# Moving the experts' final sum to ScalarE and GpSimd, one mask product to GpSimd, and the gate selectors of the first norm to a later place

## The chip, the cores and the metric

The kernel runs on one core of a Trainium2 chip. The metric is the device time of one execution in microseconds. TensorE (PE), VectorE (DVE), ScalarE (ACT), GpSimd (POOL) and SyncE (SP, which issues DMAs here) each run their own instructions in program order; they are held together by semaphores alone, so where a wait stands in an engine's order decides what queues behind it.

## The reference

The input is eight images of 32 channels by 64 by 64 pixels. What is computed, cut to what matters:

```python
xn = norm_w * instance_norm(layernorm_over_channels(x)) + norm_b
q, k, v = split(qkv_w @ xn + qkv_b)                  # 4 heads of 8, windows of 8 x 8 pixels
x = x + proj_w @ softmax(q k^T * 8**-0.5) v + proj_b
t = tokens(x)                                        # (8, 4096, 32)
n = layernorm_over_channels(t)
p, i = top_k(softmax(n @ router_w + router_b), 2)    # 2 of 8 experts
p = p / sum(p)
t = t + sum_k p[k] * (n @ expert_w[i[k]] + expert_b[i[k]])
```

The kernel multiplies each token by the gate of each expert (zero for the six that are not chosen) and sums the experts in PSUM.

## The kernel before

The 32768 pixels are cut in 16 chunks of 4 images by 512 pixels; a partition holds a channel of an image. Four chunks make a quad. There are three stretches.

**Start (0 to about 60 us).** All of x is loaded by five transfers on SP's queue, the weights by three and the gate selectors `gate_sel` by a fourth on ACT's queue. For each quad, PE subtracts the channel mean (L547), ACT squares, PE forms variances (L470), ACT takes roots (L508), DVE inverts them (`reciprocals_first`, L1085), PE spreads them over the channels (`piece_spread`, L482), and DVE multiplies (`first_norm`, L515, four instructions) and takes statistics (`statistics`, L1055). Ahead of the first quad's `first_norm` DVE runs `selectors` (L1102): it waits for `gate_sel`, and makes `regroup` (L1104), `sel_sum` (L1107) and `centre_rep` (L1112, four copies). PE uses `regroup` and `sel_sum` only at L723, after the last quad. PE then waits for `biases_ready` (L729), which DVE raises after copying three results out of PSUM bank 7 (L1133 to L1136), and begins the chunks of attention.

**Attention (about 60 to 289 us).** For every chunk PE makes scores (L596), DVE takes their maximum and subtracts it (L1149, L1152), PE turns them (L609), ACT exponentiates (L894), PE weighs the values (L626). Chunk 0 holds no earlier chunk's work. In its first half PE's order is scores, queries of chunk 1 (L566), keys of chunk 1 (L571), two turns, and only then the scores of the second half (second L596). The queries need `x_cur` of chunk 1, which ACT makes after `instance_deviation(1)` (L1000); that one waits for DVE's moments of the second group of images.

**Experts (about 289 us to the end).** For each chunk c and each half eh of the experts:

- PE makes gates for four images, two at a time (`gate_pair`, L751, banks 2 to 5) from `gate_rows`. The first pair of a chunk waits for `gates_in[c % 4]`, which stands for the transfer of that quad's gates.
- ACT copies bank 2 (`copy_gates`, L1008); POOL multiplies the first image's tokens by it (`scale`, L413); DVE multiplies the second's (L1289) and the last two's (L1292) straight from PSUM.
- PE sums the experts (`experts`, L760) in bank 6 or 7, upon the bias (L772). At eh = 0 it runs `experts(c - 1, 1)`; at eh = 1 `experts(c, 0)`. In between stand the replication of tokens for two chunks on (L737) and, in chunks 0 to 5, norms and logits for quads 2 and 3.
- DVE adds the finished sum of chunk c - 1 to the tokens (`combine`, L1267) after its two multiplications of (c, 0), and writes `out_sb`.
- The gates of quads 2 and 3 are worked out meanwhile in 30 numbered steps: DVE does most (`HALF_STEPS`), POOL 6, 14, 22, 23, 26, 27 and 29 (`LATE_POOL`), ACT the exponential, 25 and 28. Step 20 is L1226, step 21 L1228, steps 22 and 23 are L376 and L378 on POOL, step 24 is L1232 on DVE. Quad 2 takes chunks 2 to 5, quad 3 chunks 6 to 9.

SP's order in this stretch is this, and no part of the change touches it:

```python
for c in range(CHUNKS):
    if c + 3 < CHUNKS:
        repeat_tokens(c + 3)                 # 8 transfers
    if c % QUAD == 2 and c // QUAD + 1 < QUADS:
        move_gates(c // QUAD + 1)            # 4 transfers; gates_in
    sp.wait_ge(summed, c + 1)
    sp.dma_start(out_v[:, c // BANDS, c % BANDS, :], out_sb[:, c % 2, :]).then_inc(stored[c % 2], 16)
```

`summed` is raised by `combine`. So the transfers of iteration c wait until `combine(c - 1)` is done.

Of the kernel before, what the change touches and what calls it, by code (L numbers as in the profile page):

```python
# [6 lines left out]
B, C, H, W = 8, 32, 64, 64  # L7
HEADS, WS, E = 4, 8, 8
# [32 lines left out]
def metaformer_block(nc, io):  # L41
# [3 lines left out]
    with ExitStack() as ctx:  # L45
# [21 lines left out]
        v_cols = sb("v_cols", [P, 2, NW * IMG * HALVES, 2, 2, D])  # L67
        v_flat = v_cols[:].rearrange("p u g b n d -> p (u g b n d)")
        squares = sb("squares", [P, QUAD, CHUNK])
        probs = sb("probs", [P, 4, CHUNK])  # L70
# [119 lines left out]
        pool_scaled = sem("pool_scaled")  # L190
        y_step = sem("y_step")
        summed = sem("summed")
        stored = [sem(f"stored{u}") for u in range(2)]
# [54 lines left out]
        for quad in range(EARLY, QUADS):  # L248
            for h, n in ((1, 6), (4, 14), (6, 22), (7, 23), (8, 26), (8, 27), (9, 29)):
                LATE_POOL[late_half(quad, h)] += [(quad, n)]  # L250
# [51 lines left out]
        def _(pool):  # L302
# [104 lines left out]
            def scale(c, eh):  # L407

                if eh == 0:
# [4 lines left out]
                                   ALU.mult).then_inc(pool_scaled, 1)  # L414

            for c in range(CHUNKS):
                for eh in range(2):
                    h = 2 * c + eh
                    late = [(q, n) for q, n in LATE_POOL[h]]
                    for quad, n in late:  # L420
                        if n == 23:
                            gates(quad, n)
                    scale(c, eh)
                    if h == 0:
                        early(CHUNKS, 0)
                    if h == 2:
                        early(CHUNKS, 1)
                    if h == 3:
                        early(CHUNKS + 1, 0)
                    for quad, n in late:  # L430
                        if n != 23:
                            gates(quad, n)
# [86 lines left out]
        def _(pe):  # L519
# [81 lines left out]
            def turn(n, v):  # L601

                if v % 2 == 0:
                    pe.wait_ge(shifted_done, n * 4 + (v // 2 + 1))
                pe.wait_ge(exp_done, n * NW + (v + 1))
                unit, hh = v // 2, v % 2
                for b in range(IMG):
                    heads = shifted_unit[:, unit % 2, b, HALVES * hh:HALVES * hh + HALVES, :]
                    last = nc.tensor.transpose(bank[TURN_BANKS[v % 2]][:, b * P:b * P + P],  # L609
                                               heads.rearrange("p h k -> p (h k)"), const["c_ident"][:, :])  # L610
                last.then_inc(turned_ps, 1)
# [116 lines left out]
            values(0)  # L728
            pe.wait_ge(biases_ready, 1)  # L729
            chunk(0, 0, first=True)  # L730
# [34 lines left out]
            def bias(c):  # L765

                wait_past(pe, summed, c - 1)
                if c == 1:
                    pe.wait_ge(x2_done, CHUNKS + X2)
                quad = c // QUAD  # L770
                pe.wait_ge(gate_step[quad], GATE_OPS + ONE)
                nc.tensor.matmul(bank[6 + c % 2][:, :], const["c_eb"][:, c % QUAD, :],  # L772
                                 gate_f32[:, quad % 2 * CHUNK:(quad % 2 + 1) * CHUNK],
                                 start=True, stop=False, skip_group_check=True)
# [54 lines left out]
        def _(act):  # L829
            for sems in (ln1, ln2):  # L830
# [5 lines left out]
            act.dma_start(weights[:, first_cols:second_cols], io["weights"][:, first_cols:second_cols]  # L836
                          ).then_inc(spread_loaded, 16)
            act.dma_start(weights[:, second_cols:], io["weights"][:, second_cols:]).then_inc(weights_loaded, 16)
            act.dma_start(gate_in, io["gate_sel"]).then_inc(gate_in_loaded, 16)
            act.wait_ge(first_loaded, 16)  # L840
# [113 lines left out]
            def chunk(m, u, first=False, final=False):  # L954
                for hf in range(2):
# [4 lines left out]
                    if behind:  # L960
                        exps(n, back - 2)
                    if final and hf == 0:
                        square(act, ln2, EARLY, 0, centred, banks=(SHARED,))
                    elif hf == 0:
                        copy_queries(m + 1, 1 - u)
                    elif not final:
                        copy_values(m + 1, 1 - u)
# [31 lines left out]
            copy_values(0, 0)  # L999
            instance_deviation(1)  # L1000
            chunk(0, 0, first=True)
# [8 lines left out]
            def keep_tokens(c, first_bank):  # L1010
# [3 lines left out]
                for b in range(2):  # L1014
                    nc.scalar.activation(x_rep[:, slot(c), b, :], bank[first_bank + b][:, :], ACT.Copy  # L1015
                                         ).then_inc(rep_done, 1)

            exps(CHUNKS - 1, NW - 2)
            exps(CHUNKS - 1, NW - 1)
# [4 lines left out]
            for c in range(CHUNKS):  # L1024
                for eh in range(2):
                    quad, k = (c + 1) // QUAD + EARLY, (c + 1) % QUAD
                    copy_gates(c, eh)
                    if c * 2 + eh in late_act:
                        due, n = late_act[c * 2 + eh]
# [19 lines left out]
        def _(dve):  # L1049
# [52 lines left out]
            def selectors():  # L1102
                dve.wait_ge(gate_in_loaded, 16)
                nc.vector.tensor_copy(regroup[:, :].rearrange("p (r s) -> p r s", s=SPLITS + 1),  # L1104
                                      const["c_ident"][0:C, 0:C].unsqueeze(2).to_broadcast([C, C, SPLITS + 1])
                                      ).then_inc(regroup_ready, 1)
                nc.vector.tensor_reduce(sel_sum[:, :].rearrange("p (a n) -> p a n", a=2),  # L1107
                                        gate_in[0:C, :].rearrange("p (a b n) -> p a n b", a=2, b=IMG),
                                        AX.X, ALU.max).then_inc(regroup_ready, 1)
                for b in range(IMG):  # L1110
# [5 lines left out]
            reciprocals_first(0)  # L1116
            selectors()
            for quad in range(QUADS):
                first_norm(quad)
                if quad == QUADS - 2:  # L1120
# [59 lines left out]
            def gates(quad, n):  # L1180
# [44 lines left out]
                elif n == 20:  # L1225
                    one = v.tensor_tensor(small[:, p_second, :], small[:, e_gap, :], small[:, p_best, :], ALU.mult)  # L1226
                elif n == 21:
                    one = v.tensor_tensor(g(w.a), g(w.mask1), wide(p_best), ALU.mult)  # L1228
                elif n == 23:
                    one = v.tensor_tensor(w.sum, w.a, w.b, ALU.add)  # L1230
                elif n == 24:
                    one = v.transpose(w.rest, w.sum)  # L1232
# [30 lines left out]
            def combine(c):  # L1263

                dve.wait_ge(y_step, c * 2 + 2)
                wait_past(dve, stored[c % 2], c // 2 * 16)
                nc.vector.tensor_tensor(  # L1267
# [6 lines left out]

            HALF_STEPS = ((0, 1, 2), (3, 4, 5), (7, 8), (9, 10, 11, 12), (13,), (15, 16), (17, 18, 19, 20, 21), (24,))

# [7 lines left out]
            for c in range(CHUNKS):  # L1284
                wait_tokens(dve, c, 2)
                for eh in range(2):
# [10 lines left out]
                    if (c, eh) == (0, 1):  # L1297
                        dve.wait_ge(x2_done, CHUNKS - 1 + X2)
                        residual(CHUNKS - 1, bank_at=TURN_BANKS[1])
                    if eh == 0 and c >= 1:  # L1300
                        combine(c - 1)
                    if (c, eh) == (0, 1):
# [81 lines left out]
```

## Time and profile before

| what | value |
|---|---|
| median of three runs | 402.92 us |
| the three runs | 397.84, 404.67, 402.92 us |
| the profiled execution | 405.62 us, of which the span is 403.6 us |
| mean granted TensorE clock in the span | 0.964 |
| busy share of PE, DVE, ACT, POOL | 89%, 83%, 65%, 40% |

The difference between the profiled time and the span is 2.0 us. In the rows further down the first column is the start in microseconds from the span's beginning, then the duration, the engine, the line of the kernel, the operation, the tile written and the tiles read; x4 means four such instructions put together. What stands in brackets is the idle time before it and what ended it. PE's pieces overlap each other a little, and so do DVE's: the distance between starts is the better price of an instruction in a row of them.

### The profile page before, as it was taken

To read this page: it belongs to the slowest core of one execution; us is meant where nothing else is said; L and a number is where in the kernel's file an instruction comes from. 1 tells how busy PE (TensorE), PEld (TensorE's weight loads), DVE (VectorE), ACT (ScalarE), POOL (GpSimd) and SP (SyncE) were. 2 spreads that over 40 slices of the span, in tenths; PEclk is the share of its full clock that TensorE was granted. 3 is DMA by queue.
4 is the path that set the end of the run, shared out by engine and by line. 5 is a ranking of instruction groups with operands and counts; after the bars stand their busy time and mean duration, and the time that the engine had idled before them with its cause. 6 is when DMAs were issued, how large, how long until landed. Compare 5 with 4: busy or idle time off the path is not lost.

```text
span 403.6 us, 12568 instructions
## 1 busy us (share of the span) xinstructions
PE 360.6 (89%) x5318; PEld 189.1 (47%) x5318; DVE 335.2 (83%) x435; ACT 260.5 (65%) x448; POOL 162.4 (40%) x191
## 2 busy tenths in 40 slices
PE   5979689999999999999999999998898897778985
PEld 2545446665665655566566656565421221111220
DVE  1477968988988979998998979999967999996785
ACT  3735557777787798678788797775464664423331
POOL 8600000111202202378634102478593558438543
PEclk9988969999999999999999999999998999896999
DMA  8600000031000000000000100022314543533541
GB/s 306 286 2 4 2 0 3 2 74 35 4 2 4 2 3 2 2 3 2 3 2 22 37 2 3 2 59 69 87 39 107 144 123 106 139 112 96 149 139 52
DMA packets 12870, 22.49 MB, mean 56 GB/s; under 512 B 2960, under 2 KB 5136, under 8 KB 12432
## 3 DMA queue, kind: packets, MB, share of 16 engines
q1 hardware_dynamic: 12240, 19.93, 17.1%
q10 hardware_dynamic: 576, 1.77, 1.1%
q8 instruction: 42, 0.69, 0.7%
q14 instruction: 12, 0.10, 0.1%
HBM read 5.96 MB, written 4.19 MB: 25 GB/s over the span
## 4 chain that ended last, share of the span: by engine, by line
PE 57%; DVE 24%; ACT 7%; issue 5%; DMA 4%; POOL 2%; ACTq 0%; POOLq 0%; DVEq 0%
PE psum L609 13%; PE psum L626 8%; PE psum L596 6%; PE psum L634 4%; PE psum L571 4%; DMA gate_f<-gate_sel 4%; PE psum L760 3%; PE psum L566 3%; PE psum L444 3%; DVE probs L1292 3%; DVE neg_max L1149 3%; DVE window_work L1152 2%; PE psum L772 2%; PE psum L580 2%; DVE probs L1289 2%
## 5 line engine op out<-in xcount | busy, mean ns | idle before, releaser
L327 POOL TENSOR_TENSOR o_norm<-o_tok,o_rden 128x128 f32<-128x128 f32 x64 | 25.4, 418 | 178.7 <-DVE o_rden L1162 178.7
L609 PE MATMUL psum<-weights_sb,window_work 128*128 128x128 f32 x512 | 82.1, 283 | 7.0 <-DVE window_work L1152 4.0
L894 ACT ACTIVATE probs<-psum 128x512 f32<-128x512 f32 x128 | 74.8, 595 | 17.5 <-PE psum L609 15.2
L609 PEld LDWEIGHTS psum<-weights_sb,window_work 128*128 128x128 f32 x512 | 57.9, 141 | 49.6 <-issue 28.8
L1152 DVE TENSOR_TENSOR window_work<-psum,neg_max 128x1024 f32<-128x1024 f32 x64 | 78.4, 1225 | 2.2
L1149 DVE TENSOR_REDUCE neg_max<-psum 128x16 f32<-128x1024 f32 x64 | 76.8, 1199 | 4.0 <-PE psum L596 4.0
L626 PE MATMUL psum<-probs,v_cols 128*32 128x64 f32 x2048 | 54.8, 225 | 0.3 <-DVE o_tok L1160 0.2
L626 PEld LDWEIGHTS psum<-probs,v_cols 128*32 128x32 f32 x2048 | 34.8, 109 | 28.2 <-issue 24.8
L878 ACT ACTIVATE stage<-k_sb,weights_sb 128x512 f32<-128x512 f32 x64 | 44.1, 719 | 0.0
L1160 DVE STREAM_TRANSPOSE o_tok<-psum 128x512 f32<-128x512 f32 x32 | 22.9, 716 | 21.1 <-PE psum L626 21.1
L596 PE MATMUL psum<-stage 32*64 32x256 f32 x1024 | 35.8, 387 | 1.9 <-DVE proj_bias L1136 1.0
L751 PE MATMUL psum<-gate_rows,gate_sel_sb 32*128 32x512 bf16 x128 | 19.4, 400 | 12.9 <-DVE probs L1292 6.9
L413 POOL TENSOR_TENSOR probs<-stage,k_sb 128x512 f32<-128x512 f32 x16 | 20.8, 1302 | 17.1 <-ACT k_sb L1008 17.1
L751 PEld LDWEIGHTS psum<-gate_rows,gate_sel_sb 32*128 32x128 bf16 x128 | 4.9, 91 | 44.9 <-issue 30.9
L1008 ACT ACTIVATE k_sb<-psum 128x512 f32<-128x512 f32 x16 | 9.6, 598 | 25.0 <-PE psum L751 25.0
L887 ACT ACTIVATE v_cols<-psum 64x512 f32<-64x512 f32 x32 | 18.9, 591 | 8.7 <-PE psum L580 8.3
L413 POOL TENSOR_TENSOR window_work<-stage,q_sb 128x512 f32<-128x512 f32 x16 | 20.7, 1296 | 8.2 <-ACT q_sb L1008 7.4
L547 PE MATMUL psum<-stage,weights_sb 128*128 128x512 f32 x32 | 19.5, 745 | 5.0 <-DMA weights_sb<-weights 5.0
L596 PEld LDWEIGHTS psum<-stage 32*64 32x64 f32 x1024 | 19.1, 131 | 7.2 <-DVE proj_bias L1136 1.1
L566 PE MATMUL psum<-x_cur,weights_sb 128*128 128x512 f32 x32 | 18.9, 675 | 3.1 <-ACT x_cur L859 2.7
L1015 ACT ACTIVATE stage<-psum 128x512 f32<-128x512 f32 x28 | 15.1, 592 | 9.5 <-PE psum L737 9.5
L772 PE MATMUL psum<-gate_f,weights_sb 128*128 128x512 f32 x32 | 20.8, 737 | 0.0
(131 smaller groups left out, 612.4 us busy)
## 6 DMA issues: line engine op xcount, KB each, us to landing
stage<-act_all SPq DMA_DIRECT2D x144, 64.0 KB, 2.0
out<-out_sb SPq DMA_DIRECT2D x16, 256.0 KB, 2.0
stage<-in_x SPq DMA_DIRECT2D x3, 1024.0 KB, 12.4
gate_rows<-gate_parts SPq DMA_DIRECT2D x16, 128.0 KB, 2.6
weights_sb<-weights ACTq DMA_DIRECT2D x1, 811.5 KB, 11.7
stage<-in_x SPq DMA_DIRECT2D x1, 768.0 KB, 5.3
gate_f<-gate_sel ACTq DMA_DIRECT2D x1, 512.0 KB, 14.9
weights_sb<-weights ACTq DMA_DIRECT2D x1, 320.0 KB, 7.7
```

The source lines that it names most:

```text
L327: last = pool.tensor_tensor(o_norm[:, hf, :, p * 16:p * 16 + 16].rearrange("p g (b d) -> p g b d", b=2), t[:, p * 8:p * 8 + 8, :].rearrang ...
L413: pool.tensor_tensor(scaled[eh][:, 0, :], x_rep[:, slot(c), 0, :], gate_copy[eh][:, :], ALU.mult).then_inc(pool_scaled, 1)
L566: nc.tensor.matmul(bank[0][:, :], const["c_wq"][:, :], x_cur[:, :], start=True, stop=True).then_inc(q_ps, 1)
L596: last = nc.tensor.matmul(score_banks[64 * par:64 * par + 64, b, pp * 256:pp * 256 + 256], q_two[rows, u, win * TOK:win * TOK + TOK], k_he ...
L609: last = nc.tensor.transpose(bank[TURN_BANKS[v % 2]][:, b * P:b * P + P], heads.rearrange("p h k -> p (h k)"), const["c_ident"][:, :])
L626: last = nc.tensor.matmul(bank[OUT_BANK][C * b:C * b + C, at:at + TOK], v_cols[:, u, group, :, :, :].rearrange("p b n d -> p (b n d)"), pr ...
L751: last = nc.tensor.matmul(bank[2 + b][:, :], gate_sel[rows, eh * P:eh * P + P], gate_rows[rows, at:at + CHUNK], start=True, stop=True)
L772: nc.tensor.matmul(bank[6 + c % 2][:, :], const["c_eb"][:, c % QUAD, :], gate_f32[:, quad % 2 * CHUNK:(quad % 2 + 1) * CHUNK], start=True, ...
L878: one = nc.scalar.activation(k_head[:, u, h, :], k_sb[:, :], ACT.Copy, scale=const["c_masks"][:, IMG + h:IMG + h + 1])
L894: nc.scalar.activation(probs[:, w % 4, :], bank[TURN_BANKS[w % 2]][:, :], ACT.Exp).then_inc(exp_done, 1)
L1149: nc.vector.tensor_reduce(m_t, t, AX.X, ALU.max, negate=True).then_inc(max_done, 1)
L1152: nc.vector.tensor_tensor(shifted_unit[:, unit % 2, :, :, :], t, m_t.unsqueeze(3).to_broadcast([P, IMG, HEADS, TOK]), ALU.add).then_inc(sh ...
```

## The change

1. `combine` of chunks 0 to 14 leaves DVE. ACT copies the finished bank to a new tile `y_sb` (`keep_sum(c - 1)`, after `copy_gates(c, 1)`), and POOL adds it to the tokens (`combine(c - 1)`, after `scale(c, 1)`) and raises `summed`. PE's bias waits for the copy (`y_kept`), not for the sum. The last chunk's stays on DVE, behind `summed` of chunk 14. `y_sb` lies in the place of `v_cols`, which attention no longer needs.
2. Step 21 of quads 2 and 3 goes from DVE to POOL, in the half of step 20 behind `scale`. Step 22 moves one half on, in front of step 23 and of that half's `scale`.
3. `selectors` is cut in two. `regroups` (`regroup`, `centre_rep`) stays ahead of the first norm and waits for no `gate_sel`; `sel_sum` comes in front of `first_norm` of quad 1. The transfer of `gate_sel` goes ahead of the last one of the weights.
4. PE begins chunk 0 of attention once the last `first_norm` is done; the wait for `biases_ready` moves to the second turn, which writes bank 7. ACT runs `instance_deviation(1)` inside chunk 0, behind `x_cur` of chunk 1 and in front of the copy of its queries.

```diff
+        y_sb = v_flat[:, 0:2 * CHUNK].rearrange("p (u n) -> p u n", u=2)
@@
-            for h, n in ((1, 6), (4, 14), (6, 22), (7, 23), (8, 26), (8, 27), (9, 29)):
+            for h, n in ((1, 6), (4, 14), (6, 21), (7, 22), (7, 23), (8, 26), (8, 27), (9, 29)):
@@ gpsimd
+            def combine(c):
+                pool.wait_ge(y_kept, c + 1)
+                wait_past(pool, stored[c % 2], c // 2 * 16)
+                pool.tensor_tensor(
+                    out_sb[:, c % 2, :].rearrange("p (y win x) -> p win y x", win=NW, y=WS),
+                    y_sb[:, c % 2, :].rearrange("p (win y x) -> p win y x", win=NW, y=WS),
+                    act_all[:, c * CHUNK:c * CHUNK + CHUNK].rearrange("p (win y x) -> p win y x", win=NW, y=WS),
+                    ALU.add).then_inc(summed, 1)
@@
-                        if n == 23:
+                        if n in (22, 23):
                             gates(quad, n)
                     scale(c, eh)
+                    if eh == 1 and c >= 1:
+                        combine(c - 1)
@@ tensor, turn(n, v)
+                if n == 0 and v == 1:
+                    pe.wait_ge(biases_ready, 1)
@@
-            pe.wait_ge(biases_ready, 1)
+            pe.wait_ge(ln1["normed"], CHUNKS + NORMED)
             chunk(0, 0, first=True)
@@ bias(c)
-                wait_past(pe, summed, c - 1)
+                wait_past(pe, y_kept, c - 1)
@@ scalar
+            act.dma_start(gate_in, io["gate_sel"]).then_inc(gate_in_loaded, 16)
             act.dma_start(weights[:, second_cols:], io["weights"][:, second_cols:]).then_inc(weights_loaded, 16)
-            act.dma_start(gate_in, io["gate_sel"]).then_inc(gate_in_loaded, 16)
@@ chunk
+                    if first and hf == 0:
+                        instance_deviation(1)
@@
-            instance_deviation(1)
             chunk(0, 0, first=True)
@@
+            def keep_sum(c):
+                act.wait_ge(y_step, c * 2 + 2)
+                wait_past(act, summed, c - 1)
+                nc.scalar.activation(y_sb[:, c % 2, :], bank[6 + c % 2][:, :], ACT.Copy).then_inc(y_kept, 1)
@@
                     copy_gates(c, eh)
+                    if eh == 1 and c >= 1:
+                        keep_sum(c - 1)
@@ vector
             def selectors():
                 dve.wait_ge(gate_in_loaded, 16)
+                nc.vector.tensor_reduce(sel_sum[:, :].rearrange("p (a n) -> p a n", a=2),
+                                        gate_in[0:C, :].rearrange("p (a b n) -> p a n b", a=2, b=IMG),
+                                        AX.X, ALU.max).then_inc(regroup_ready, 1)
+
+            def regroups():
@@
-            selectors()
+            regroups()
             for quad in range(QUADS):
+                if quad == 1:
+                    selectors()
                 first_norm(quad)
@@ gates(quad, n)
-                elif n == 21:
-                    one = v.tensor_tensor(g(w.a), g(w.mask1), wide(p_best), ALU.mult)
-                elif n == 23:
-                    one = v.tensor_tensor(w.sum, w.a, w.b, ALU.add)
@@ combine(c), now for the last chunk alone
-                wait_past(dve, stored[c % 2], c // 2 * 16)
+                dve.wait_ge(summed, c)
+                dve.wait_ge(stored[c % 2], c // 2 * 16)
@@
-            HALF_STEPS = (..., (17, 18, 19, 20, 21), (24,))
+            HALF_STEPS = (..., (17, 18, 19, 20), (24,))
@@
-                    if eh == 0 and c >= 1:
-                        combine(c - 1)
```

## Rows read from the trace of the kernel before

**Rows 1.** Busy time by stage: PE, PEld, DVE, ACT, POOL, granted clock, DMA share, GB/s

```profile
20.00:44.00 24.00, 19.90 (x398) 12.66 (x387) 18.47 (x37) 10.47 (x23) 0.90 (x2) 0.86 0.01 3
44.00:60.00 16.00, 11.21 (x152) 6.56 (x148) 11.73 (x18) 9.17 (x15) 0.00 (x0) 0.79 0.00 1
60.00:290.00 230.00, 220.97 (x4116) 139.99 (x4114) 204.96 (x248) 178.88 (x305) 81.84 (x111) 1.00 0.07 18
...
360.00:370.00 10.00, 7.10 (x28) 1.62 (x28) 7.58 (x13) 2.91 (x5) 6.88 (x6) 0.71 0.29 81
```

**Rows 2.** Timeline of the start, the first norm of quads 0 to 2

```profile
15.89 2.01 PE L482 MATMUL psum<-rstd_first,spread_pieces 32*128 32x64 f32 x64
...
17.63 1.97 DVE L1107 TENSOR_REDUCE sel_sum<-gate_f 32x256 f32<-32x1024 f32 x1
...
19.53 1.91 DVE L1112 COPY centre_rep<-weights_sb 32x128 f32<-32x128 f32 x4
...
20.78 1.98 PE L547 MATMUL psum<-stage,weights_sb 128*128 128x512 f32 x4
...
21.46 2.48 DVE L515 TENSOR_TENSOR act_all<-act_all,psum 128x512 f32<-128x512 f32 x4
...
25.05 0.53 DVE L1085 RECIPROCAL rstd_first<-std_pair 128x64 f32<-128x64 f32 x1
25.50 1.22 DVE L1055 BATCH_NORM_STATS2 stats<-act_all 128x6 f32<-128x512 f32 x2
...
35.86 0.14 DVE L1129 TENSOR_SCALAR qb_scaled<-weights_sb 128x1 f32<-128x1 f32 x1
...
38.05 2.47 DVE L515 TENSOR_TENSOR act_all<-act_all,psum 128x512 f32<-128x512 f32 x4
```

**Rows 3.** Timeline of attention's chunk 0

```profile
47.34 1.12 PE L596 MATMUL psum<-stage 32*64 32x256 f32 x32 [0.99 <-DVE proj_bias L1136]
...
50.11 0.29 ACT L853 ACTIVATE inst<-moments,weights_sb 128x1 f32<-128x1 f32 x1 [2.45 <-DVE moments L1060]
...
53.58 1.22 DVE L1152 TENSOR_TENSOR window_work<-psum,neg_max 128x1024 f32<-128x1024 f32 x1
...
54.02 2.08 PE L571 MATMUL psum<-x_cur,weights_sb 128*128 128x512 f32 x2 [0.78 <-ACT stage L865]
...
57.43 1.12 PE L596 MATMUL psum<-stage 32*64 32x256 f32 x32
```

**Rows 4.** Groups by line, 290 us to the end: count, busy, mean ns, idle before

```profile
L413 POOL TENSOR_TENSOR probs<-stage,k_sb 128x512 f32<-128x512 f32 x16 | 20.8, 1302 | 17.1 <-ACT k_sb L1008 17.1
...
L1267 DVE TENSOR_TENSOR out_sb<-psum,act_all 128x512 f32<-128x512 f32 x16 | 11.0, 685 | 5.7 <-PE psum L760 5.6
...
L376 POOL TENSOR_TENSOR x_win<-x_win,small 128x512 f32<-128x512 f32 x3 | 3.2, 1076 | 7.8 <-DVE x_win L1228 7.7
...
L1228 DVE TENSOR_TENSOR x_win<-x_win,small 128x512 f32<-128x512 f32 x2 | 1.4, 692 | 0.1
```

**Rows 5.** Timeline of SP's DMA issues in the experts' stretch

```profile
369.47 0.34 SPq L297 DMA_DIRECT2D out<-out_sb  x1
369.90 4.95 SPq L282 DMA_DIRECT2D stage<-act_all  x8
374.90 2.57 SPq L270 DMA_DIRECT2D gate_rows<-gate_parts  x4
```

**Rows 6.** The page's DMA issues: count, KB each, median us to landing

```profile
gate_rows<-gate_parts SPq DMA_DIRECT2D x16, 128.0 KB, 2.6
```

**Rows 7.** Timeline of the experts' stretch, chunks 8 to 12

```profile
357.04 1.58 DVE L1217 TENSOR_TENSOR x_win<-x_win,small 128x512 f32<-128x512 f32 x1
...
361.93 0.22 DVE L1226 TENSOR_TENSOR small<-small 128x64 f32<-128x64 f32 x1
...
365.41 0.71 DVE L1232 STREAM_TRANSPOSE std_pair<-x_win 128x512 f32<-128x512 f32 x1 [0.80 <-POOL x_win L378]
...
378.70 0.39 PE L751 MATMUL psum<-gate_rows,gate_sel_sb 32*128 32x512 bf16 x2 [0.65 <-DVE probs L1292]
```

More of the change, by code:

```diff
@@ L191, in metaformer_block @@
         y_step = sem("y_step")
+        y_kept = sem("y_kept")
         summed = sem("summed")
@@ L430, in _ @@
                     for quad, n in late:
-                        if n != 23:
+                        if n not in (22, 23):
                             gates(quad, n)
@@ L1106, in selectors @@
                                       ).then_inc(regroup_ready, 1)
-                nc.vector.tensor_reduce(sel_sum[:, :].rearrange("p (a n) -> p a n", a=2),
-                                        gate_in[0:C, :].rearrange("p (a b n) -> p a n b", a=2, b=IMG),
-                                        AX.X, ALU.max).then_inc(regroup_ready, 1)
                 for b in range(IMG):
@@ L1273, in _ @@
             divide(CHUNKS - 1, 1)
-            HALF_STEPS = ((0, 1, 2), (3, 4, 5), (7, 8), (9, 10, 11, 12), (13,), (15, 16), (17, 18, 19, 20, 21), (24,))
+            HALF_STEPS = ((0, 1, 2), (3, 4, 5), (7, 8), (9, 10, 11, 12), (13,), (15, 16), (17, 18, 19, 20), (24,))
             def steps(c, eh):
```

## The prediction, made before the change was run

> **What bounds the kernel now.** I read the busy time by stage first [rows 1]. From 60 to 290 us PE is busy 221 of 230 us at the full clock, and the change has nothing there; whatever the start saves is carried through unchanged. In the two stages ahead of it PE is busy 20 of 24 and 11 of 16 us, with a mean granted clock of 0.86 and 0.79: these are the stages in which engines wait for each other. Next comes the timeline of the start [rows 2]. PE has spread the reciprocals of quad 0 at 15.89 + 2.01 = 17.90, but the multiplication that waits for them starts at 21.46, because DVE is at `sel_sum` and `centre_rep`. The reader is to see a DVE that is behind for a reason that has nothing to do with the norm. In chunk 0 [rows 3] the first scores are released by DVE's `proj_bias`, and the second scores come at 57.43, though the scores' place in PSUM was free when the L1152 of 53.58 ended, at 54.80; PE was at the keys and the turns, at half clock.
>
> The experts' stretch has two regimes. While the gates of quads 2 and 3 are worked out (chunks 2 to 9) DVE is nearly always busy, and the chain of waits runs through its lines. From chunk 10 on the chain alternates between PE and DVE, and `combine` lies in a gap: DVE idled 5.7 us ahead of its 16 instances, for PE's L760 [rows 4]. A shorter DVE helps only in the first regime.
>
> **The start, part by part.** Walk DVE with the new order [rows 2]. `centre_rep` (1.91) now runs from about 15.1 to 17.1, while DVE waited for `gate_sel` before. The first norm starts at 17.9 and ends at 20.4 (2.48); two statistics (1.22) and the reciprocal (0.53) bring it to 22.2. PE is at L547 until 20.78 + 1.98 = 22.76, then spreads quad 1 until 24.8 (2.0, at the full clock). DVE does two statistics (23.4) and `sel_sum` (1.97, 25.4), so `sel_sum` costs 0.6 us of the path here. Norm of quad 1 until 27.8, two statistics and a reciprocal until 29.6, two statistics until 30.8. From there to the norm of quad 2 it was 38.05 - 35.86 = 2.2 us. So that norm starts at 33.0 in place of 38.05: **5.0 us**. PE no longer idles between 22.8 and its next spreading, and I count it at the full clock. Below nothing this part can't go, except if the transfer of the weights, now last on its queue, landed after 30.8; from 20 us on the DMA engines were busy for 1% of the time [rows 1].
>
> In chunk 0 DVE comes to the scores 5.0 earlier, since its own order is the same. The second scores then wait for the later of DVE, 54.80 - 5.0 = 49.8, and PE. PE's first scores start as soon as the norm is done, its queries no longer wait for the moments, and only its keys do. The deviation was at 50.11 and is now at 45.1; with its 0.29 and 0.7 for the copy of the queries the keys begin at 46.1. They took 2.08 at half clock and take half of it at the full one. The turns behind them need DVE's first difference, 2.4 before 49.8, and about 1.2 at the full clock. So PE is free at 48.7, or at half clock at about 50.6. So the second scores come at 49.8 to 50.6 instead of 57.43: 6.8 to **7.6 us** in all from the start, of which I take 7.2. The lower bound is 5.0, where PE would stay as late against DVE as before.
>
> **The experts: what DVE gives up.** `combine` is 0.60 us of DVE in a row of them (0.685 by itself [rows 4]), and step 21 the same (0.692). In chunks 2 to 9 that is 8 x 0.6 + 2 x 0.6 = 6.0 us at most. Chunk 2 is set by PE and ACT. The copies of ACT (0.6 each) lie in ACT's idle time. In chunks 10 to 14 the saving is 0.
>
> **What POOL takes on.** POOL shows no such addition; the nearest rows are `scale` with 1.30 us and L376 with 1.08 [rows 4]. I take 1.30 for `combine` and 1.08 for step 21. Steps 21, 22 and 23 are now a chain on POOL: from step 20's end, 362.15, to step 24, 365.41, it was 3.26 us [rows 7], of which DVE's step 21 was 0.6. With 1.08 and its handover for 0.6 it becomes 3.6, and DVE stands still for it longer: +0.35 us in each of the two quads.
>
> Then the port. L1217 with two inputs in SBUF took 1.58 us in the midst of a POOL multiplication, where an instruction of its shape takes 0.69 [rows 4, 7]. Fifteen more POOL additions can fall on it. In my walk they fall on steps 2, 5 or 16 three or four times, 0.3 to 0.7 us each. The Trainium skill (SBUF — State Buffer, "Who interferes with whom") says that a DVE instruction with two SBUF inputs and a GpSimd one that reads SBUF exclude each other for the whole instruction; the row agrees. By that rule the loss is at most 15 x 1.3 us, by the row the 0.9 us of L1217 a time; most of it is hidden here behind what follows.
>
> **The wait that the change adds.** The part that I think decides: `combine` raises `summed`, and SP's next transfers are queued behind that wait. Before, `combine(c - 1)` was done soon after `experts(c - 1, 1)`. Now it ends after `scale(c, 1)`, half a chunk later, some 4 us. Behind it on SP stand the output (0.34), eight repetitions of tokens (4.95) and, at c = 2, 6 and 10, the four transfers of the next quad's gates. From the issue of the output to that of the gates it was 374.90 - 369.47 = 5.43 us [rows 5], and to landing 2.6 more [rows 6]: 8.05 us after `combine`. PE can't begin chunks 4, 8 and 12 without them. The repeated tokens themselves have three chunks of time, and stay hidden by 1 us or more.
>
> For chunk 12: the walk brings step 20 of quad 3 to 362.15 + 0.8 (below). Steps 21 to 23 take 3.6. POOL then has seven operations in a row before `summed` is raised: `scale(9, 1)`, `combine(8)`, `scale(10, 0)`, steps 26 and 27, `scale(10, 1)`, `combine(9)`. At 1.25 each (between 1.08 and 1.30) these are 8.75, so `combine(9)` ends at 375.3. Plus 8.05 gives 383.35 for the gates. PE's second pair of gates, 0.35 behind the first, comes at 383.7; before it was at 378.70 [rows 7]. That is **+5.0 us** at chunk 12, and everything behind it is a chain of PE and DVE that keeps it.
>
> Chunks 4 and 8 have a chunk of DVE-bound time in between, so their gates come 2 to 4 us late for PE but hardly for DVE. PE then is behind, and DVE's second half of chunks 4 and 8 waits for it. This eats the 6.0 us of DVE: I find DVE 0.5 late in chunk 4, 1.4 in chunk 8, and step 20 of quad 3 0.8 late. The bounds: if neither stall reached DVE, step 20 would come 1.8 us earlier than before, and chunk 12 would still be late by 5.0 - 2.6 = 2.4 us; if both did in full, 2 us later and 6.5 us.
>
> **The clock.** From 360 to 370 us the granted clock had a mean of 0.71 [rows 1], that is, a part at 1.2 GHz, after PE had idled. In the new kernel PE idles about 4 us ahead of chunk 12. A stretch at half clock behind it costs PE's chain there 1 to 2 us; I take 1.3.
>
> **The sum**, against the profiled 405.6 us: - 7.2 + 5.0 + 1.3 = 404.7. This execution is 2.7 us above the median of the runs. Some of that is clock lost in chunks 8 to 10, which the new kernel hides behind its wait; so I take half of it off: **403.4 us**, no change within what can be told.
>
> **Rivals.**
> 1. SP's queue has slack that I don't see, and only DVE's relief counts. For it speaks that DVE is the busiest engine in chunks 2 to 9. Against it stands the order of the code, and that the gates of chunk 12 were issued at 374.90 and landed at 377.5, only 1.2 before PE's second pair: there was no slack before. It gives 402.9 - 7.2 - 4 to 6, 390 to 392. Chance 0.14.
> 2. Slower: each of the three waits for gates puts PE at half clock, and for long. The stretch at 360 to 370 shows 0.71, some 6 us at half. Three of these cost 3 us each: 404.7 - 1.3 + 9 = 412. It decides from the point where PE idles over 3 us at chunks 4 and 8 too and PE, not DVE, sets what follows. Chance 0.08.
> 3. The start doesn't give what it says: DVE is early, but PE or ACT sets the path and half clock stays in chunk 0. Then 402.9 - 3 + 6 = 406. Chance 0.13.
> 4. The forecast: the start gives about 7, the experts take about 6 back. Chance 0.65, by itself 398 to 408.
>
> Below 394.9 counts as faster, above 411 as slower (2%, about what can be told from no change). From the cases: faster 0.14, same 0.77, slower 0.09. The range leaves out rivals 1 and 2: 396.5 to 409.5.
>
> **What would show it.** In the new profile the norm of quad 0 starts near 17.9 and the second scores near 50. POOL holds 15 additions of some 1.3 us. SP's transfers of gates for chunk 12 are issued 5.4 us behind the output, and PE's L751 waits for that DMA by several microseconds at chunk 12, by some at 4 and 8. If PE never waits for gates, rival 1 is right. If the clock is at half in several places behind 300 us, it is rival 2.

## The result, and the profile after

The changed kernel took 407.63 us (median of 6 runs, 406.64 to 409.42), the kernel before 403.27 (6 runs, 397.84 to 405.62). The ratio is 1.0155, with a 95% interval of 1.0102 to 1.0208: slower, by more than the noise, where the forecast was 403.4 and no change. The ratio is not the quotient of the two medians, which is 1.0108: by the medians the loss is 4.4 us, by the ratio 6.2. Ratio and medians part by up to half a per cent in the experiments too, so a difference of a few microseconds is good to 1 or 2. The profiled execution took 406.94 us, with a span of 404.9.

From the page of the changed kernel, the busy time, and the group of the gates' products (its L767 is L751 of before, L415 is L413, L776 is L760, L788 is L772):

```profile
PE 360.6 (89%) x5318; PEld 187.4 (46%) x5318; DVE 325.6 (80%) x418; ACT 267.3 (66%) x463; POOL 184.3 (46%) x208
...
L767 PE MATMUL psum<-gate_rows,gate_sel_sb 32*128 32x512 bf16 x128 | 17.4, 411 | 16.1 <-DMA gate_rows<-gate_parts 8.9
```

DVE has 9.6 us less work than before and the kernel is longer. PE now idles 8.9 us for the transfers of gates. The timeline of the start of the changed kernel:

```profile
18.17 2.48 DVE L529 TENSOR_TENSOR act_all<-act_all,psum 128x512 f32<-128x512 f32 x4 [1.23 <-PE psum L496]
...
32.12 2.47 DVE L529 TENSOR_TENSOR act_all<-act_all,psum 128x512 f32<-128x512 f32 x4
...
48.92 1.12 PE L610 MATMUL psum<-stage 32*64 32x256 f32 x32
```

The norm of quad 2 starts at 32.12 (before: 38.05 [rows 2]) and the second scores of chunk 0 at 48.92 (before: 57.43 [rows 3]). The first gates of the experts come at 279.8 in place of 288.6. So the start gave 8.8 us between these two traces, and the experts' stretch, from the first gates to the end of the span, grew from 115.0 to 125.1 us.

What waits in that stretch, from the waits of the changed kernel after 280 us (total, times, longest, in us; PEld is PE's weight load, which waits ahead of the product, so its 12.1 and PE's 8.9 are the same three waits and don't add up):

```profile
DVE probs L1315 <- PE psum L767: 21.0, 11, 4.0
...
PEld psum L767 <- DMA gate_rows<-gate_parts: 12.1, 3, 5.4
...
PE psum L767 <- DMA gate_rows<-gate_parts: 8.9, 3, 4.5
DVE window_work L1315 <- PE psum L767: 7.5, 5, 5.1
```

Three waits, as three chunks need new gates. DVE, which was to be relieved, waits for gates in its turn. The third, for chunk 12, with SP's issues around it and what PE does behind it:

```profile
360.08 1.27 POOL L415 TENSOR_TENSOR probs<-stage,k_sb 128x512 f32<-128x512 f32 x1
...
367.48 1.28 POOL L422 TENSOR_TENSOR out_sb<-v_cols,act_all 128x512 f32<-128x512 f32 x1
368.72 1.15 POOL L384 TENSOR_TENSOR gate_parts<-x_win,gate_parts 128x512 bf16<-128x512 f32 x1
...
368.79 0.34 SPq L299 DMA_DIRECT2D out<-out_sb  x1
369.22 4.94 SPq L284 DMA_DIRECT2D stage<-act_all  x8
374.21 2.57 SPq L272 DMA_DIRECT2D gate_rows<-gate_parts  x4
...
376.84 0.61 PE L767 MATMUL psum<-gate_rows,gate_sel_sb 32*128 32x512 bf16 x4 [4.53 <-DMA gate_rows<-gate_parts]
377.25 1.91 PE L753 MATMUL psum<-act_all,centre_rep 32*128 32x512 f32 x4
...
379.08 1.94 PE L776 MATMUL psum<-probs,we_centred 128*32 128x512 f32 x8
...
380.95 2.08 PE L788 MATMUL psum<-gate_f,weights_sb 128*128 128x512 f32 x2
```

GpSimd's sum of chunk 9 (L422) ends at 368.76, the output is issued at once, and 8.05 us after that issue PE has its gates. The gates themselves were finished by L384 at 369.87, and their transfers are issued at 374.21: 4.3 us behind SP's repetitions of tokens. Behind the wait PE's groups take nearly twice their time: L776 takes 1.94, and 1.06 at the full clock. The stages by granted clock, changed kernel (columns as in [rows 1]):

```profile
312.00:319.00 7.00, 7.00 (x20) 1.84 (x18) 3.71 (x5) 3.73 (x7) 3.74 (x4) 0.57 0.40 113
...
370.00:376.00 6.00, 1.67 (x13) 0.29 (x12) 1.82 (x2) 1.08 (x2) 3.60 (x3) 1.00 0.47 119
376.00:384.00 8.00, 7.16 (x30) 1.61 (x30) 2.36 (x3) 2.29 (x5) 1.27 (x1) 0.57 0.57 155
```

Between 370 and 376 PE is busy 1.67 of 6 us; the stage behind it has a mean clock of 0.57, nearly all of it the lower level of 1.2 GHz. The same stands behind the wait of chunk 4. In narrower windows of this trace the granted clock is at the lower level from 311.3 to 318.1, 335.2 to 342.0, 345.4 to 348.8, 362.5 to 365.9 and 376.1 to 382.9, about 27 us. The first, third and last stretch, 17 us, come with the three waits for gates; the second comes before the wait of chunk 8 and, like the fourth, behind PE's waits for DVE. Before, the experts' stretch had about 14 us at half clock.

### The profile page after: what moved, and what is told of

The parts are those of the page before. It is cut to its first block, busy times and chain, and to the rows that moved or that the text cites. A ratio compares the mean times of both kernels' runs of the same rounds, so it can differ in the third digit from the quotient of the medians.

```text
span 404.9 us, 12597 instructions
## 1 busy us (share of the span) xinstructions
PE 360.6 (89%) x5318; PEld 187.4 (46%) x5318; DVE 325.6 (80%) x418; ACT 267.3 (66%) x463; POOL 184.3 (46%) x208
## 4 chain that ended last, share of the span: by engine, by line
PE 57%; DVE 12%; POOL 8%; ACT 8%; issue 6%; DMA 4%; SPq 4%; ACTq 0%; POOLq 0%; DVEq 0%
PE psum L625 13%; PE psum L642 8%; PE psum L610 6%; PE psum L650 4%; PE psum L585 4%; SPq L284 3%; PE psum L458 3%; PE psum L580 3%; PE psum L776 3%; DVE neg_max L1178 3%; POOL probs L415 3%; PE psum L561 3%; DVE window_work L1181 2%; POOL out_sb L422 2%; PE psum L594 2%
## 5 line engine op out<-in xcount | busy, mean ns | idle before, releaser
L767 PE MATMUL psum<-gate_rows,gate_sel_sb 32*128 32x512 bf16 x128 | 17.4, 411 | 16.1 <-DMA gate_rows<-gate_parts 8.9
L415 POOL TENSOR_TENSOR probs<-stage,k_sb 128x512 f32<-128x512 f32 x16 | 20.8, 1301 | 16.4 <-ACT k_sb L1025 16.4
L1315 DVE TENSOR_TENSOR probs<-stage,psum 128x512 f32<-128x512 f32 x16 | 10.9, 683 | 21.0 <-PE psum L767 21.0
L767 PEld LDWEIGHTS psum<-gate_rows,gate_sel_sb 32*128 32x128 bf16 x128 | 4.3, 92 | 48.1 <-issue 27.8
L415 POOL TENSOR_TENSOR window_work<-stage,q_sb 128x512 f32<-128x512 f32 x16 | 20.8, 1300 | 10.6 <-issue 6.2
L776 PE MATMUL psum<-probs,we_centred 128*32 128x512 f32 x128 | 20.5, 718 | 3.2 <-DVE window_work L1315 2.1
L788 PE MATMUL psum<-gate_f,weights_sb 128*128 128x512 f32 x32 | 22.2, 782 | 0.0
```

Of the source, the lines that this page charges most:

```text
L415: pool.tensor_tensor(scaled[eh][:, 0, :], x_rep[:, slot(c), 0, :], gate_copy[eh][:, :], ALU.mult).then_inc(pool_scaled, 1)
L776: last = nc.tensor.matmul(bank[6 + c % 2][32 * b:32 * b + 32, :], we_centred[:, eh, :], scaled[eh][:, b, :], start=False, stop=(eh == 1), ...
```

## The experiments

The theory is the queue on SP: `summed` comes later, the gates' transfers stand behind it, PE waits, and the clock falls behind each wait. The rivals are the chain of steps 21 to 23 on GpSimd, GpSimd's load or the shared port, and a start whose gain is lost later.

**The start's part alone.** The kernel before with points 3 and 4 of the change.

> The kernel before with the start's part of the change alone (selectors cut in two, the transfers swapped, the two waits of chunk 0 moved). Theory: what the start saves is carried through the attention unchanged, and the loss is all in the experts' stretch. In the new kernel's trace the experts begin 8.8 us earlier, so this kernel takes 403.3 - 8.8 = 394.5 us, 392 to 397. Rival, that the gain of the start is swallowed further on whatever the experts do (a fixed wait, a clock that falls later): 400 to 404.

Measured: 397.11 us (4 runs) against 402.69, ratio 0.9838 (0.9764 to 0.9913). Its experts' stretch is 115.1 us in the trace, as before. The gain is carried through. It is 5.6 us between the medians and 6.5 by the ratio, not 8.8: the profiled execution of before is above its median, with two stretches at half clock in its start, so the pair of traces overstated it. The traces of the next two kernels, whose start is the old one, bear this out: their first gates come at 285.2 and 287.3, not 288.6.

**The sum on GpSimd alone.** The kernel before with point 1.

> The kernel before with the move of the sum to ScalarE and GpSimd alone. Theory (SP's transfers queued behind the later sum): PE waits for gates by 2 us at chunks 4 and 8 and by 4.5 at chunk 12, with the clock at half behind each, and the experts' stretch gains 8 to 10 us: 410 to 414. Rival, that it is step 21 on GpSimd which makes the chain late: 403 to 405.

Measured: 415.35 us (5 runs), ratio 1.029 (1.0215 to 1.0364). PE waits 8.8 us for the gates in this trace, its weight loads 12.3; before, PE did not wait for them and its weight loads 0.8. This one part holds the loss, 12.7 us between the medians, a little more than the 8 to 10 expected. The experts' stretch of its profiled execution, the fastest of the five, is 123.3 us, 8.3 longer.

**Step 21 on GpSimd alone.**

```diff
-            for h, n in ((1, 6), (4, 14), (6, 22), (7, 23), ...
+            for h, n in ((1, 6), (4, 14), (6, 21), (7, 22), (7, 23), ...
```

> The kernel before with step 21 on GpSimd alone (step 22 moved with it). Theory: the chain of steps 21 to 23 is 0.35 us longer in each of two quads, and DVE is 0.6 shorter: within 1 us of before, 402.5 to 404.5. Rival, that this chain is what makes the gates late: 406 or more.

Measured: 406.46 us (10 runs) against 402.69, ratio 1.006 (1.0018 to 1.0103). The loss is 3.8 us between the medians, which is outside what I expected and in the rival's range of 406 or more, and 2.4 by the ratio. The rival's reason is not in the trace: PE waits 0.2 us for gates. What the chain costs is small against the 10 us of the experts' stretch. DVE idles in front of step 24 for 3.9 us in all, where it was 1.6: the 1.1 us on GpSimd costs more than the 0.6 us that DVE is rid of.

**The late store.** The changed kernel, with the store of a chunk one iteration later on SP:

```diff
                 if c % QUAD == 2 and c // QUAD + 1 < QUADS:
                     move_gates(c // QUAD + 1)
-                sp.wait_ge(summed, c + 1)
-                sp.dma_start(out_v[...], out_sb[:, c % 2, :]).then_inc(stored[c % 2], 16)
+                if c >= 1:
+                    store(c - 1)
+            store(CHUNKS - 1)
```

> The changed kernel with one edit: SP stores chunk c - 1 in iteration c, behind the repetitions and the gates' transfers, so that these no longer wait for the sum of the chunk before. Nothing is taken off GpSimd. Theory (SP's order is the cause): no wait for gates of over 1 us is left, the half clock behind them goes, and the time is below that of the start alone by what DVE gives up less the port: 389 to 395. Rival, that GpSimd's load and the shared port are the cause: GpSimd's chain up to the last step of the gates is as late as before, and the time stays above 401.

Measured: 396.24 us (4 runs), ratio 0.9805 (0.9736 to 0.9875). GpSimd does the same work, and 11 us are back, though not the 389 to 395 that I expected. Chunk 12's gates in this kernel:

```profile
364.22 1.28 POOL L427 TENSOR_TENSOR out_sb<-v_cols,act_all 128x512 f32<-128x512 f32 x1
365.46 1.16 POOL L389 TENSOR_TENSOR gate_parts<-x_win,gate_parts 128x512 bf16<-128x512 f32 x1
...
366.65 2.56 SPq L272 DMA_DIRECT2D gate_rows<-gate_parts  x4
...
369.26 0.87 PE L772 MATMUL psum<-gate_rows,gate_sel_sb 32*128 32x512 bf16 x4 [0.20 <-DMA gate_rows<-gate_parts]
```

The gates are issued 1.15 us after the same sum ends, not 5.4, and PE waits 0.20: they go out at 366.65, as soon as the last step of the gates (L389) ends at 366.62. The order on SP is the cause, as far as the waits go. But the time is that of the start alone: the relief of DVE brought next to nothing (114.2 us of experts' stretch against 115.1).

**Gates first.** The changed kernel with `move_gates` ahead of `repeat_tokens(c + 3)`, both still behind the sum.

> The changed kernel with the gates' transfers in front of the eight repetitions (still behind the sum of the chunk before). Theory (what counts is how long the gates are queued on SP behind the sum, 5.4 us of 8.05): the transfers land 4.95 us earlier, all three waits vanish, and the time is that of the late store, 395 to 398. Rival, that the repetitions' delay costs as well: 399 to 403.

Measured: 398.73 us (8 runs), ratio 0.99 (0.986 to 0.9939). Taking only the eight repetitions out of the gates' way recovers some 9 of the 11 us, and in the trace PE waits 0.2 us for the gates, as in the late store. The median lies between my 395 to 398 and the rival's 399 to 403. It is 2.5 us above the late store's, and the intervals of the two ratios overlap; that the repetitions' delay makes this difference isn't shown.

**PE kept busy in the waits.** The changed kernel, SP's order as it is:

```diff
                     if eh == 0:
+                        if c % QUAD == 0 and c > 0:
+                            pe.wait_ge(gate_copied, c * 2)
+                            for _ in range(4 if c == 12 else 2):
+                                nc.tensor.matmul(bank[2][:, :], const["c_centre"][:, :], act_all[:, 0:CHUNK],
+                                                 start=True, stop=True)
                         pe.wait_ge(gates_in[c % QUAD], c // QUAD * 16 + 16)
```

> The changed kernel in which PE, ahead of its wait for the gates of chunks 4, 8 and 12, runs 2, 2 and 4 products of 128x512 into bank 2 (about 1.0 us each, results overwritten), so that it is busy in most of a wait that it has anyway. Theory: part of the loss is the half clock behind the waits (2.8 us behind chunk 12's alone); the stretches at half clock behind chunks 4 and 12 go and the time falls by 2 to 5 us, to 403 to 405.5. Rival, that the half clock is hidden by other engines and the waits alone cost: within 1 us of 407.6.

Measured: 401.77 us (10 runs, 399.42 to 404.87), ratio 0.995 (0.9912 to 0.9989). Eight products whose results are thrown away make the kernel 5.9 us faster than the changed one, more than the 2 to 5 expected. The same stages by clock:

```profile
312.00:319.00 7.00, 7.00 (x42) 1.79 (x34) 6.22 (x8) 6.23 (x13) 5.46 (x5) 1.00 0.48 140
...
370.00:376.00 6.00, 5.13 (x30) 1.39 (x32) 1.87 (x3) 1.80 (x4) 1.29 (x1) 1.00 0.65 178
376.00:384.00 8.00, 6.70 (x46) 1.49 (x42) 6.06 (x8) 4.33 (x8) 5.70 (x5) 1.00 0.43 117
```

and PE around chunk 12, with the extra products at L833 (the trace holds two instructions for each):

```profile
367.65 3.70 PE L833 MATMUL psum<-act_all,weights_sb 128*128 128x512 f32 x8
372.22 0.40 PE L767 MATMUL psum<-gate_rows,gate_sel_sb 32*128 32x512 bf16 x4 [0.87 <-DMA gate_rows<-gate_parts]
...
373.40 1.06 PE L776 MATMUL psum<-probs,we_centred 128*32 128x512 f32 x8
```

The wait for gates is still there (3.70 of products and 0.87 idle; over the three waits 7.7 and 2.2, against 8.9 idle), but the clock stays at its upper level of 2.4 GHz, and L776 takes 1.06 where it took 1.94. About 10 us at half clock are left in this kernel's experts' stretch, of 27. So of the 11 us between the changed kernel and the late store about 6 come with the lower clock, and about 5 with the waits themselves. By the traces' experts' stretches (125.1, 118.0, 114.2) it is 7 and 4, by the ratios 8 and 6.

The lower clock also made the gates late. From the first gates of the experts to the end of step 20 of quad 3 it is 73.6 us before and 76.7 in the changed kernel, and with PE kept busy 72.2, as in the late store. Step 20 in the changed kernel, then with PE kept busy (first gates at 279.79 and 279.43):

```profile
356.25 0.23 DVE L1255 TENSOR_TENSOR small<-small 128x64 f32<-128x64 f32 x1
```

```profile
351.44 0.22 DVE L1260 TENSOR_TENSOR small<-small 128x64 f32<-128x64 f32 x1
```

**Where DVE's relief went.** In the late store DVE's L1320 waits 16.4 us for PE's gates; the same instruction waited 6.6 with DVE doing the sum. One row of the waits of each, first the late store, then the start alone:

```profile
DVE probs L1320 <- PE psum L772: 14.9, 8, 3.5
```

```profile
DVE probs L1296 <- PE psum L753: 5.3, 7, 1.7
```

The time that DVE is rid of, it waits. Three kernels ask whether step 21, the store, or GpSimd's work is what PE waits for. First, the late store with steps 21 and 22 where they were before:

> The kernel with late store (396.2), with step 21 back on DVE (and step 22 back in its half). The relief of DVE brought nothing there: the experts' stretch is 114.2 us against 115.0. Theory: DVE stands still 1.8 and 1.9 us in front of step 24 for steps 21 to 23 on GpSimd, and step 21 gives nothing: 394.5 to 396. Rival, that the port is what eats the relief (L1225 took 1.69 us in place of 0.75): step 21 makes no difference, within 0.7 of 396.2.

Measured: 397.13 us (4 runs), ratio 0.9831 (0.9783 to 0.9878): not told from the late store. The wait in front of step 24 fell from 3.8 to 1.6 us, and the time didn't. It is above the 394.5 to 396 that I expected. In this surrounding, then, step 21 is worth nothing that can be told either way; this is near the rival's number (0.9 us off, where it allowed 0.7), but its reason, the port, is at most a small part (below).

Then the start alone, with the late store and the sum on DVE:

> The start's part alone, with the late store, the sum and step 21 on DVE. Theory: without the sum on GpSimd SP isn't what the gates wait for, save 1 us at chunk 12; the same as the start alone, 396 to 397.5, and with this the move of the sum is worth the difference to the late store with it: 0 to 1 us. Rival, that the late store itself is the gain: 393 to 395.

Measured: 397.32 us (4 runs), ratio 0.9846 (0.9797 to 0.9894), the same as the start alone. The late store is worth something only where the sum is late.

Then the late store without GpSimd's additions. In this kernel and the next the tokens of chunks 0 to 14 are not added, and zeros go out for them; both also fill `out_sb` with zeros once at the start.

```diff
-                pool.tensor_tensor(out_sb[...], y_sb[...], act_all[...], ALU.add).then_inc(summed, 1)
+                pool.memset(out_sb[:, c % 2, 0:8], 0.0).then_inc(summed, 1)
```

> The late store, with GpSimd's addition of chunks 0 to 14 left out (the outputs of these chunks are zeros; a write of 8 columns raises the semaphore instead). It takes 15 x 1.25 us off GpSimd and its reads off the port. Theory: the relief of DVE brought nothing because PE's own chain is what DVE then waits for (its L1320 waited 16.4 us for gates, against 6.6 in the start alone), and GpSimd's load is hidden: 395 to 396.5. Rival, that GpSimd's additions (late products for PE, blocked DVE instructions) ate the relief: 391 to 394.

Measured: 392.25 us (4 runs), ratio 0.9719 (0.967 to 0.9767). My expectation was wrong and the rival right: GpSimd's fifteen additions cost some 4 us. Here DVE's relief arrives: step 20 of quad 3 ends 68.3 us behind the first gates, against 73.8 in the start alone and 72.2 with the additions.

Then with GpSimd held by writes that read nothing:

```diff
+                for _ in range(2):
+                    follow(pool.memset(out_sb[:, c % 2, :], 0.0))
+                pool.memset(out_sb[:, c % 2, :], 0.0).then_inc(summed, 1)
```

> As the one without additions, but GpSimd writes zeros three times over the same 128x512 (about 1.3 to 1.5 us, nothing read; the sums of chunks 0 to 14 are left out). It holds GpSimd as long as the addition, without its reads. If the port is the cause this is as fast as the kernel without additions and faster than the late store; if GpSimd's time is, as slow as the late store; if neither, all three within 1 us, which is what I expect: 395 to 397.

Measured: 395.87 us (4 runs), ratio 0.9813 (0.9771 to 0.9854), as slow as with the additions (396.24); the number is in my range, but not for my reason, that all three would be alike. GpSimd's groups over the experts' stretch, of this kernel and of the one with the short write:

```profile
L429 POOL MEMSET out_sb<- 128x512 f32 x30 | 15.8, 525 | 0.9
...
L430 POOL MEMSET out_sb<- 128x512 f32 x15 | 7.9, 525 | 0.9
```

```profile
L428 POOL MEMSET out_sb<- 128x8 f32 x15 | 1.6, 105 | 0.0
```

The writes hold GpSimd 1.58 us a time, somewhat longer than an addition (1.34 in the late store), and read nothing. So GpSimd's time alone is enough for the loss, by the medians. By the traces' experts' stretches it is 113.3 us with the fill, 114.2 with the additions and 110.3 with neither. Where it lands is seen in the waits of this kernel:

```profile
PE psum L780 <- POOL window_work L421: 4.3, 6, 2.5
```

It is the next half's `scale`, late behind the fill, that PE's sum of the experts waits for. In the kernel with the short write the waits have no such row for `window_work`. With the additions the row is there, but with 1.9 us in three waits, so that it accounts for about half of the 4 us; where the rest lands isn't shown. The port isn't excluded as a smaller part: as the fill is 0.24 us longer than the addition, some of what the port costs could be hidden in that.

**PE kept busy in the late store.** One or two of the same products in four halves in which PE idled ahead of a fall of the clock.

> The late store, with one or two products of 128x512 that PE runs into the bank of its next sum in the halves (2, 0), (6, 0), (7, 1) and (10, 0), where it would idle ahead of the three stretches at half clock (3.4, 3.4 and 6.8 us of the experts' stretch). Theory: PE's chain sets the pace there, so the half clock costs up to half of its 13.6 us: 390 to 394, and faster than both kernels by over 2%. Rival, that DVE and GpSimd hide it, or that the extra products delay as much as they save: 395 to 398.

Measured: 397.13 us (6 runs), ratio 0.9833 (0.9792 to 0.9874). The clock at half fell to two stretches of 3.4 us ahead of the end, and the time didn't move: the 390 to 394 that I expected was wrong, and the rival's 395 to 398 right. There the products bring nothing; whether half clock there is hidden by DVE and GpSimd, or the products delay what they save, I haven't told apart. No kernel here is told from the late store as faster, except with work left out.

## Why the prediction was right or wrong

**The start** was walked right. The norms came at 18.17 and 32.12 (said: 17.9 and 33.0), the second scores at 48.92 (49.8 to 50.6). The term was 7.2 us; the pair of traces shows 8.8 and the run with this part alone 5.6 to 6.5. Rival 3, which gave the start 3 us, is out.

**DVE's relief.** I gave 6.0 us at most and let the stalls of chunks 4 and 8 eat it. The late store has no such stall; step 20 of quad 3 is 1.4 us early there, and at the end next to nothing of it is left. GpSimd's time takes most of it: without the additions the stretch is 110.3 us, with them 114.2. I had costed the additions at nothing apart from the delay of `summed` and the port, though I had counted seven GpSimd operations without a gap. Behind such a chain the next `scale` is late too, and PE waits for it.

**Step 21.** Said 0.35 us in each quad; the run with it alone says 0.2 to 1% in all, 1 to 4 us. The wait in front of step 24 grew by 2.3 us in the two quads together, of which DVE's lighter work gives back 1.2. Too low, and small.

**The port.** Two rows of DVE in the changed kernel, of one shape:

```profile
329.94 0.69 DVE L1215 STREAM_TRANSPOSE std_pair<-std_two 128x512 f32<-128x512 f32 x1
...
331.25 1.68 DVE L1220 SCALAR_TENSOR_TENSOR x_win<-std_two,weights_sb,raw_logits 128x512 f32<-128x512 f32 x1
```

L1220 reads two tiles of 128x512 in SBUF, and here it lies beside a multiplication of GpSimd that reads two (L382, 331.23 to 332.39); the median of its four runs is 0.70. The one that reads a single tile, L1215, kept its time beside another multiplication of GpSimd (L415, 330.00 to 331.27). That is the exclusion which the Trainium skill (SBUF — State Buffer, "Who interferes with whom") states, and the trace agrees. It stays a small term: GpSimd held without reads costs nearly as much (395.87 against 396.24).

**The queue on SP** was the part that I thought decides, and it does. The seven GpSimd operations took 8.68 us (said: 8.75), and from the sum to the gates it was 8.08 (said: 8.05). But the gates' own last step (L384) ends 1.1 us behind the sum, which the walk left out; what the queue adds is the 4.3 us between that step and the issue, and this is what the late store takes away.

**The step that failed** is the clock. The sum has it with 1.3 us, behind chunk 12 alone, and the walk of chunks 4 to 9 is at the full clock, although the same text has PE without gates at chunks 4 and 8. The clock there was left to rival 2, with a chance of 0.08 and on the condition that PE idles over 3 us. PE idled 2.2 us at each, and half clock followed:

```profile
310.64 0.40 PE L767 MATMUL psum<-gate_rows,gate_sel_sb 32*128 32x512 bf16 x4 [2.18 <-DMA gate_rows<-gate_parts]
...
344.56 0.40 PE L767 MATMUL psum<-gate_rows,gate_sel_sb 32*128 32x512 bf16 x4 [2.16 <-DMA gate_rows<-gate_parts]
```

Two terms were too small by it. Step 20 of quad 3 was to be 0.8 us late. It ended at 356.48, which with the start's 8.8 stands against 362.15: 3.1 late, more than the 2 us that I gave as the bound. With PE kept busy it is 1.4 early, counted from the first gates. So the +5.0 for chunk 12 was 7.3: 383.35 was forecast without the start, and 376.84 + 8.8 = 385.6 came. And the stretch behind chunk 12's gates grew by the rest of the 10.1 us, 2.8, where 1.3 was said. In the traces, then, 405.6 - 8.8 + 7.3 + 2.8 = 406.9. (The last term is what is left over, so this sum shows where the time lies and doesn't test anything.) Rival 2 had the mechanism: half clock in several places behind 300 us. It priced it at 9 us, and PE kept busy gave 5.9.

Another slip is in the bounds of that walk: a step 20 that is 2 us late in place of 0.8 makes chunk 12 late by 6.2 us, not 6.5.

**The median.** I took off half of the 2.7 us between the profiled execution and the median for clock lost in chunks 8 to 10, which the new kernel was to hide behind its wait. It didn't: the changed kernel has 6.8 and 3.4 us at half clock there too. Its profiled execution is below its own median. This 1.4 was no term of the kernel.

The measured time lies in the range (396.5 to 409.5), and it is less than 2% slower; the range left rival 2 out, whose mechanism came true, so that the time lies there is partly luck. The direction was not forecast, and it is beyond the noise.

## What to carry to other kernels

When work goes to another engine, look at who waits for its semaphore and what is queued behind that waiter, not at its data alone: here a store's wait held up twelve transfers that had nothing to do with the store. Put the wait last in such a queue. Waits of TensorE like these three (2.2, 2.2 and 4.5 us) are to be costed with the lower clock behind them (here about 6 us more in all), and not the longest of them alone. In the late store taking half clock away brought nothing, so the price is due where TensorE sets the pace behind the wait; that this is the difference is my reading, not shown. And time taken off the busiest engine is worth only what the next chain lets through, here the one of GpSimd's products and PE's sums.

## What was not expected of the hardware

Eight products of about 1.0 us each, of no use to the result, made the changed kernel 5.9 us faster (407.63 to 401.77), as they held the granted clock at its upper level through the three waits; five such products in the late store changed nothing that can be told (396.24 and 397.13). An addition of 128x512 on GpSimd took 1.28 us with its permuted operands (the median of fifteen), where a plain product, L415, took 1.27 (the median as well).
